# Turning the gathered rows of the routed tiles by a transposing DMA instead of on TensorE

## The reference

```python
x = x + xattn(_layernorm(x), ctx_1024, pos, ...)
# ffn, on h = _layernorm(x), T = 2048 tokens of H = 512, I = 352, E = 16, K = 2
def _swiglu(x, a, b, c):
    return silu(x @ a.T) * (x @ b.T) @ c.T
shared_output = _swiglu(h, shared_w1, shared_w3, shared_w2)
scores = sigmoid(h @ gate_w.T)
_, topk_idx = top_k(scores + bias, K)
sel = take_along_axis(scores, topk_idx, axis=1)
gating = sel / sel.sum(axis=-1, keepdims=True)      # combine[t, e] holds these
for e in range(E):
    routed_output += combine[:, e:e + 1] * _swiglu(h, w1[e], w3[e], w2[e])
x = x + shared_output + routed_output
```

## Time and profile before

| | |
|---|---|
| median of 3 runs | 740.51 us (737.42 to 745.31) |
| profiled execution | 740.43 us, its span 738.7 us |
| PE busy | 681.3 us (92%) |
| DVE, ACT, POOL busy | 525.3, 397.6, 366.1 us (71%, 54%, 50%) |
| granted TensorE clock, mean | 0.976 |
| shared tiles / routed tiles | about 373 to 479 us / 479 to 725 us of the span |

### The profile page before, as it was taken

How to read it: one execution, slowest core, us unless ns; L and a number is a source line. 1 busy time by engine, 2 the same in 40 slices (tenths; PEclk the granted TensorE clock), 3 DMA queues, 4 the chain that set the end, 5 groups by cost and what they waited for, 6 DMA issues and landing times.

```text
span 738.7 us, 20567 instructions
## 1 busy us (share of the span) xinstructions
PE 681.3 (92%) x7616; PEld 436.3 (59%) x7616; DVE 525.3 (71%) x992; ACT 397.6 (54%) x666; POOL 366.1 (50%) x439
## 2 busy tenths in 40 slices
PE   3389999999999999998489998999999999999992
PEld 1156666666666666666245665666666666666661
DVE  5968888888888888876537772467676666767671
ACT  4255666665666666665521111366666656666661
POOL 5455556655556665542100001145776557777662
PEclk9789999999999999999979999999999999999997
DMA  9610111000011110000113256258568875555952
GB/s 300 222 48 9 37 38 39 34 21 35 21 35 35 35 35 28 28 29 31 59 57 100 72 182 225 73 145 250 97 192 239 254 199 94 98 94 78 278 121 31
DMA packets 37601, 73.88 MB, mean 100 GB/s; under 512 B 3920, under 2 KB 8048, under 8 KB 37552
## 3 DMA queue, kind: packets, MB, share of 16 engines
q1 hardware_dynamic: 26736, 48.81, 19.2%
q0 software_dynamic: 8800, 20.73, 14.9%
q10 hardware_dynamic: 2016, 3.67, 1.7%
HBM read 69.85 MB, written 22.81 MB: 125 GB/s over the span
## 4 chain that ended last, share of the span: by engine, by line
PE 83%; DVE 6%; DMA 4%; issue 3%; POOL 2%; ACT 1%; POOLq 0%; SPq 0%; DVEq 0%; ACTq 0%
PE p_sc L712 13%; PE p_qk L692 13%; PE p_sc L692 12%; PE p_v L486 8%; PE p_qk L486 7%; PE p_pv L586 5%; PE p_st L534 4%; PE p_pv L589 4%; PE p_sc L566 3%; PE p_sc L549 3%; PE p_pv L596 2%; PE p_tr L678 2%; PE p_v L699 2%; PE p_sc L569 2%; DMA xeT<-xn2T_dram 2%
## 5 line engine op out<-in xcount | busy, mean ns | idle before, releaser
L809 ACT ACTIVATE prob<-p_sc 128x512 f32<-128x512 f32 x128 | 71.4, 601 | 58.8 <-PE p_sc L569 58.8
L1073 DVE TENSOR_REDUCE negmax<-p_sc 128x4 f16<-128x512 f32 x128 | 82.7, 685 | 8.6 <-PE p_sc L549 8.0
L924 ACT CAST hiddenT<-p_v 128x384 f16<-128x384 f32 x54 | 25.9, 479 | 108.7 <-PE p_v L699 108.7
L712 PE MATMUL p_sc<-used_twice,hiddenT 128*128 128x512 f16 (+1 forms) x342 | 80.1, 379 | 0.0
L1192 DVE TENSOR_TENSOR hidden<-p_sc,act_g 128x352 f32<-128x352 f32 x55 | 28.8, 524 | 68.5 <-PE p_sc L692 47.0
L1467 POOL COPY from_at<-from_rows 128x1 uint32 (+1 forms) x40 | 33.0, 825 | 89.0 <-DVE from_rows L1309 85.8
L692 PE MATMUL p_sc<-used_twice,xeT 128*128 128x352 f16 x468 | 76.2, 313 | 0.0
L692 PE MATMUL p_qk<-used_twice,xeT 128*128 128x352 f16 x468 | 76.2, 312 | 0.0
L1487 POOL DMA_INDIRECT out<-prob,to_at x38 | 67.8, 1786 | 11.0 <-issue 10.1
L1100 DVE SCALAR_TENSOR_TENSOR used_twice<-w,used_twice 128x704 f16<-128x704 f32 x80 | 67.7, 887 | 2.5
L692 PEld LDWEIGHTS p_sc<-used_twice,xeT 128*128 128x128 f16 x468 | 45.8, 98 | 24.0
(11 more groups left out here) (186 smaller groups left out, 1551.3 us busy)
## 6 DMA issues: line engine op xcount, KB each, us to landing
w<-e SPq DMA_DIRECT2D x20, 1408.0 KB
w<-e SPq DMA_DIRECT2D x20, 512.0 KB
out<-stream SPq DMA_DIRECT2D x17, 256.0 KB, 2.1
xn_dram<-xn_parts SPq DMA_DIRECT2D x16, 256.0 KB, 2.0
xn2T_dram<-xn2T SPq DMA_DIRECT2D x16, 256.0 KB, 2.0
w<-e SPq DMA_DIRECT2D x20, 192.0 KB
stream<-x SPq DMA_DIRECT2D x1, 3584.0 KB, 16.8
xeT<-xn2T_dram ACTq DMA_DIRECT2D x14, 256.0 KB, 2.7
```

Of the source, the lines that this page charges most:

```text
L712: mm = pe.matmul(p_y[u][:], hiddenT[0:k, h_part, c, :], w[0:k, w_part, c, :], start=(c == 0 and h_part + w_part == 0), stop=(c == len(ICH) ...
L809: act.activation(prob[:, c % RING, :], p_scored(c)[:], ACT.Exp, scale=SCALE).then_inc(exp_ready, 1)
L1073: dve.tensor_reduce(negmax[:, c % 2, at:at + CH], p_scored(c)[:].rearrange("p (h t) -> p h t", t=P), AX_X, ALU.max, negate=True).then_inc( ...
```

## The change

`rows_transpose` on PE and `xeT_copy` on ACT are gone. In the place of `xeT_copy`, ACT now runs `rows_turn`: it waits until the gather into `xe[u]` has landed and until PE is through with the `gate_up` that last read this slot of xeT, makes a one-column copy into `carrier_act`, and issues one transposing DMA from `xe[u]` in SBUF to `xeT[u]` in SBUF, eight blocks of 128 x 128. `gate_up` waits for the DMA's semaphore `xT_loaded[u]`, as it does in the shared pairs. POOL's gather into a slot of `xe` waits for the landing of the turn, where it waited for PE's transposes. At the end ACT waits for the last turns.

```diff
-            def rows_transpose(n, u, j):
-                pe.wait_ge(sems.xe_gathered[u], (j - (SHARED - 1)) * 16)
-                for a in range(2):
-                    for c in range(KC):
-                        mm = pe.transpose(p_xT[:, a, c, :], xe[:, u, a, c * P:(c + 1) * P], ident16[:])
-                mm.then_inc(sems.xeT_done, 1)
-
             def gate_up(n, u, j, par, kind):
 
-                if kind == "shared":
-                    pe.wait_ge(sems.xT_loaded[u], j * 16 + 16)
-                else:
-                    pe.wait_ge(sems.xeT_ready, n - (B - 1))
+                pe.wait_ge(sems.xT_loaded[u], j * 16 + 16)
+                if kind == "routed":
                     pe.wait_ge(lo13, split_no(j) * KC)
...
-                    if kinds[1] == "routed":
-                        rows_transpose(n + 2, u, j + 1)
                     down(n, u, j, par, kinds[0])
...
-            def xeT_copy(n, u):
-                act.wait_ge(sems.xeT_done, n - (B - 1))
+            def rows_turn(n, u, j):
+                act.wait_ge(sems.xe_gathered[u], (j - (SHARED - 1)) * 16)
                 act.wait_ge(sems.u_done, n - 1)
-                act.copy(xeT[:, u], p_xT).then_inc(sems.xeT_ready, 1)
+                act.copy(carrier_act[:, u:u + 1], minus_half[:])
+                act.dma_start_transpose(xeT[:, u].rearrange("p a c t -> p (a c) t"), xe[:, u].rearrange("p a d -> p (a d)")).then_inc(sems.xT_loaded[u], 16)
...
-                    xeT_copy(n + 2, 0)
+                    rows_turn(n + 2, 0, j + 1)
...
-                    xeT_copy(n + 3, 1)
-
-            pairs(pair, act)
+                    rows_turn(n + 3, 1, j + 1)
+                else:
+                    for u in range(SUB):
+                        act.nop().then_inc(sems.xT_loaded[u], 16)
+
+            used = pairs(pair, act)
+            for u in range(SUB):
+                act.wait_ge(sems.xT_loaded[u], used * 16 + (SHARED + 1) * 16)
+            act.copy(carrier_act[:, SUB:SUB + 1], minus_half[:])
...
                 if later(j, SHARED + 1):
-                    pool.wait_ge(sems.xeT_done, (j - SHARED) * SUB + (u - 1))
+                    pool.wait_ge(sems.xT_loaded[u], j * 16)
```

More of the change, by code:

```diff
@@ L67, in __init__ @@
         self.xe_gathered = [sem(f"xe_gathered{n}") for n in range(2)]
-        self.xeT_done = sem("xeT_done")
-        self.xeT_ready = sem("xeT_ready")
         self.g_done = sem("g_done")
@@ L113, in build @@
         ones16 = sb("ones16", [P, P], F16)
-        carrier_dve, carrier_pool = sb("carrier_dve", [P, 1]), sb("carrier_pool", [P, 2 * SUB + 1])
+        carrier_dve, carrier_act, carrier_pool = sb("carrier_dve", [P, 1]), sb("carrier_act", [P, SUB + 1]), sb("carrier_pool", [P, 2 * SUB + 1])
         minus_half = sb("minus_half", [P, 1])
```

## The result

| | before | after |
|---|---|---|
| median (lowest to highest) | 739.13 us, 4 runs (737.42 to 745.31) | 789.76 us, 4 runs (786.47 to 798.14) |
| profiled execution's span | 738.7 us | 788.4 us |
| ratio, 95% interval | | 1.0679 (1.0624 to 1.0735) |
| granted TensorE clock, mean | 0.976 | 0.942 |

The forecast was 829 us, the range 757 to 985, and slower with a chance of 0.90. The medians differ by 50.6 us where 89 were forecast.

The account below looks back on a forecast made before the run. PE, busy 92% of the span, was taken as the bound. With the turning DMA landing in 5.0 us a pair takes 17.28 us against 12.60; 19 x 4.68 = 89 us on 740.4 gives 829 us, range 757 to 985.

Parts of the forecast that it names:

- What bounds the kernel, and what is saved: Routed tiles: PE is the bound with transposes on its path; removing 40 groups of 0.45 us saves at most 18.0 us.
- The closed chain: Routed steps: a late `gate_up` delays the next `gate_act` and issue, so each step costs its full length, nothing caught up.
- The time from `gate_up` to the issue: ACT, routed steps: `gate_act`, weight splits and small copy precede the DMA issue; 4.01 us at u = 0, less at u = 1.
- L = 3.5: Turning DMA's time from issue to landing in the routed stretch if turning is free; 19 x 1.68 = 32 us slower.
- rival 1: Turning is free, the DMA landing in 3 to 4 us like a plain one: 772 us, band 749 to 791, chance 0.20.
- L = 5.0: Turning DMA's time from issue to landing: 3.5 us plain plus 1.5 for turning; a pair lasts 17.28 us, not 12.60.
- 31 ns a piece: Most that a small DMA piece costs, from the `pos_sb` load; 2.0 us for the turn's 64 pieces on an engine.
- What is at no cost: Routed pairs: ACT issue up to about 2 us, POOL's later gather, SP's loads and the last turns' waits add nothing.
- another reason: POOL's waits for adding DMAs before the change, 42.0 us in 29 times, showed it late for a reason left unnamed.
- The clock: Routed part: clock near 1.00, falling near 3.4 us of PE idling; above L = 5.2, 3 us a step; a fall means wrong.
- Rival 3: Turning is heavy, landing over 6.5 us: 951 us at 8.2, up to 1065 with the clock down; chance 0.24.
- Rival 2: The DMA is hidden because SBUF to SBUF without HBM lands sooner than 2.5 us: 727 us or 722, chance 0.05.

Follow-up runs that it names:

- e1: Changed kernel with the weight loads of the routed pairs from the third on cut to three pieces of one partition: 725.77 us, 0.9783 of the kernel before.
- e3: Changed kernel with a plain DMA of the same 256 KB, 128 rows of 2 KB, in place of the turning one: 764.93 us, ratio 1.0286.
- e4: Changed kernel with each turn moved up by half a pair on ACT, 8.0 us before PE needs it: 762.76 us, ratio 1.0252.
- e11: Kernel before with only slot 1's tiles turned by DMA, issued half a pair earlier than in the changed kernel; slot 0 stays on PE: 757.20 us, ratio 1.0166.
- e12: e11 with one more wait on SP, the w13 load waiting until the turn in flight has landed: 756.83 us, ratio 1.0169.
- e2: Kernel before with the weight loads of the routed pairs from the third on cut to three pieces of one partition: 738.88 us, ratio 0.9959.
- e9: Changed kernel with each adding DMA of a routed tile replaced by a plain DMA of 1 KB: 752.58 us, ratio 1.0102.
- e10: Changed kernel with half of each weight load from the third routed pair on: 747.08 us, ratio 1.0057.

## Why the prediction came out as it did

**What bounds the kernel, and what is saved.** Right in the main. PE's transposes were on the path; with the loads away their removal gives 13.1 us of the 18.0. The sum put PE's work at 5.85 us in both steps. In every second one DVE's low parts now end last, which I had at nothing, and the step is 6.03.

**The closed chain.** Right in its form: each late turn costs its full length, nothing is caught up, and PE's waits for DMA xeT<-xe are the loss. I expected it in 35 to 38 steps; the profile puts 15 of PE's waits there (50.7 us). So the mechanism holds in the pairs with a load and not in the others.

**The time from `gate_up` to the issue: wrong.** I counted the splits and the small copy, 4.01 and 3.17 us. Measured at full clock it is 2.1 in both steps (740.42 to 742.50, 749.35 to 751.51), since the issue doesn't wait for what stands ahead of it on ACT. PE therefore leaves the turn 5.86 - 2.1 = 3.7 us, not 1.8 and 2.6. With L = 3.5 this alone makes rival 1 a gain, as e1 shows.

**L = 5.0: right as a mean, wrong for nearly every step.** Alone the turn takes 3.1 us (e1), 3.6 in the middle of the changed kernel. The 18 turns of the pairs with a load take 6.7 in the mean, the other 20 take 3.3, both from the start of the issue to the release of PE or POOL: (20 x 3.3 + 18 x 6.7) / 38 = 4.9. The two terms of the estimate were too high for a quiet stretch: the plain copy of e3 lands in 2.5 in the middle, not 3.5, and the turn alone 0.6 us later than that, not 1.5, though my 31 ns a piece was near: 10.8% x 16 x 788.4 us less before's 1.7% x 16 x 738.7 is 1161 us for the 42,240 added packets, 27 ns each, 1.8 us for the 66 of an engine. And I used one middle value for the stretch, where the rows held two: the earlier trace rows had 5.40 and 7.59 us beside loads, and I named them and then averaged.

**The two errors partly cancelled.** With the true 2.1 us to the issue and L = 5.0 everywhere a pair is 14.3 us, and the forecast would have been 773, below the 789.8 measured: a mean hides that a turn of 13 us costs its full excess and one of 3 us gives nothing back. The count to the issue, too long by 1.9 and 1.1 us a step, put 57 us on top. That the time lies within the range is in part luck. It also lies just inside the band that I gave to rival 1 (749 to 791), whose mechanism it is not.

**What is at no cost.** ACT's issue of 1.25 us is hidden, as said. That POOL's queue "has more room, not less" holds for the changed kernel (10.3 us of waiting for adds, had 42.0); in e4, e11 and e12, where the turns are less in the way, POOL's adds and gathers are what fails. The "another reason" for POOL being late before is the weight loads (e2).

**The clock.** It fell, which I had named as a sign of being wrong: 0.92 in the routed stretch where 1.00 was forecast, and at least 10.5 us of the 50. Six `gate_up` start at the lower clock, four after PE was idle for 7.5 to 10.0 us behind turns of over 11 us, and two after 3.2 and 2.5 us (498.67 and 515.78). At 749.35, after 2.9 us, the clock stayed full, so the 3.4 us that I read from the earlier trace rows did not divide the cases. Mostly for the same reason PE is busy by only 2.7 us less, where I expected 18.

**The rivals.** Rival 1 goes with the Trainium skill ("Advanced Engine Details and Errata", X-Bar Transpose), by which TRN2 transposing DMAs are as fast as regular ones. Alone that is nearly so here (3.1 us in e1 against 2.5 in the middle of e3), but not beside a load, where e3 is 25 us faster. The 1309 ns a block of the Trainium skill ("VectorE: DVE Perf Modes", The three transpose paths), taken eight times, is out: 3.1 us for eight blocks. Rival 3 (L over 6.5, and the clock down) was right for the turns beside loads alone. Its upper bound was also added up loosely: the clock down in a third of 38 steps is 38 us, and 951 + 38 = 989, not 985. Rival 2's gain comes without the loads (2.2% in e1), but not by its mechanism: no turn landed under 3.0 us, and it is the earlier issue that leaves room for it.

What stays open is why a load, a DMA of 1,024 pieces and an adding DMA together give 11 to 14 us. e3, e9 and e10 show that all three are needed for it; how the engines share their time among them is not shown.

## What to carry to other kernels

A transfer that replaces on-chip work must be weighed in the stretches where the DMA engines are busiest, not by its median: here it gained 0.6 us in each of ten pairs and cost 6.2 us in each of nine. Ask what else is in flight when it is issued, and how many pieces it has: beside a weight load 1,024 of them took up to 11.5 us, 128 with the same bytes up to 8.9. When the engines are 85% busy and their transfers wait for each other, don't count on an earlier issue or another order to make the room; here neither did. And when the bound of a step gets shorter, look for what ends just behind it, as DVE's low parts did here.

## What was not expected of the hardware

- A DMA issued from ACT starts while earlier ACT instructions still run: 610.34, with `carrier_act` ahead of it in the program at 611.05.
- The issue of the turning DMA takes 1.25 us of ACT's queue, a plain one between the same tiles 0.47, and one of 1,024 pieces 0.60.
- The busy share of the DMA engines can rise while the bytes fall: 0.96 at 180 GB/s in a pair with turns and a load, 0.85 at 249 GB/s before.
- A turn of 256 KB from SBUF to SBUF lands in 3.0 to 3.8 us with nothing large beside it, 11 to 14 us beside a weight load and an adding DMA.
